# Attention stage: four extra quarters of exponentials, maxima transposed after a group's first quarter, first batch's projection before the last group

## The reference

```python
q, k, v = proj(w_q), proj(w_k), proj(w_v)             # of layernorm(x); (2, 32, 512, 16)
scores = einsum('bhqd,bhkd->bhqk', q, k) / sqrt(16)
attn = softmax(scores, axis=-1)
x = x + einsum('bso,eo->bse', heads(attn @ v), w_o)
x = x + experts(layernorm(x))                          # 2 of 8 experts a token, 800 wide
```

## Time and profile before

| | |
|---|---|
| median of 3 runs | 570.74 us (569.82 to 576.18) |
| the profiled execution | 570.89 us, span 569.0 us |
| TensorE clock granted, mean | 0.986 |
| TensorE busy | 544.3 us, 96% |
| VectorE busy | 390.8 us, 69% |
| ScalarE busy | 323.3 us, 57% |
| attention loop, first V product to last o_raw | 98.6 to 275.7 us |

### The profile page before, as it was taken

One profiled execution on the slowest core, in us unless ns is written; L12 is line 12 of the kernel. 1 busy time (PEld: TensorE's weight loads), 2 busy tenths in 40 slices (PEclk: granted clock), 3 DMA queues, 4 the chain that ended last, 5 costly groups with the idle time before them and its releaser, 6 DMA issues.

```text
span 569.0 us, 9750 instructions
## 1 busy us (share of the span) xinstructions
PE 544.3 (96%) x3504; PEld 394.2 (69%) x3504; DVE 390.8 (69%) x728; ACT 323.3 (57%) x479; POOL 129.3 (23%) x154
## 2 busy tenths in 40 slices
PE   8999999999999999999997999999999999999991
PEld 6886664333333333333766998999999999999991
DVE  6914656999999999961678787663828466576650
ACT  4322114777777777787245473656656575657540
POOL 4300111000230212451301023234240321332202
PEclk9999999999999999999998999999999999999996
DMA  8290367837567752002394878295574757486122
GB/s 327 98 112 0 54 84 87 112 45 89 70 89 90 86 70 88 21 12 87 104 372 169 286 245 290 48 319 110 209 216 140 271 140 291 82 298 169 49 31 36
DMA packets 31116, 78.19 MB, mean 137 GB/s; under 512 B 9692, under 2 KB 10972, under 8 KB 26586
## 3 DMA queue, kind: packets, MB, share of 16 engines
q1 hardware_dynamic: 25770, 68.84, 46.1%
q0 software_dynamic: 5296, 8.69, 8.2%
HBM read 53.11 MB, written 9.32 MB: 110 GB/s over the span
## 4 chain that ended last, share of the span: by engine, by line
PE 79%; DVE 9%; DMA 4%; issue 3%; POOL 2%; ACT 1%; SPq 0%; POOLq 0%; ACTq 0%
PE ps L707 16%; PE ps L709 15%; PE ps L708 15%; PE ps_o L719 9%; PE ps L738 8%; DVE neg_max L1378 6%; PE ps_m L738 4%; DMA q_hi<-o_norm 1%; POOL o_norm L623 1%; PE ps L750 1%; PE ps_m L972 1%; DMA x<-x 1%; PE ps_o L707 1%; PE ps L1007 1%; PE ps L1010 1%
## 5 line engine op out<-in xcount | busy, mean ns | idle before, releaser
L1165 ACT ACTIVATE probs_t<-ps 128x1024 f32<-128x1024 f32 x128 | 124.0, 1022 | 42.0 <-PE ps L750 42.0
L1378 DVE TENSOR_REDUCE neg_max<-ps 128x1 f32<-128x512 f32 x171 | 111.7, 684 | 10.4 <-PE ps L738 7.9
L707 PE MATMUL ps<-xgT_hi,w_hi 128*128 128x256 f32 (+7 forms) x384 | 110.7, 288 | 1.2 <-DVE xgT_lo L1636 1.2
L708 PE MATMUL ps<-xgT_lo,w_hi 128*128 128x256 f32 (+7 forms) x384 | 109.7, 286 | 0.0
L709 PE MATMUL ps<-xgT_hi,w_lo 128*128 128x256 f32 (+7 forms) x384 | 109.7, 286 | 0.0
L738 PE MATMUL ps<-k_stack,q_stack 48*128 48x512 f32 x171 | 72.9, 461 | 2.9 <-issue 0.6
L707 PEld LDWEIGHTS ps<-xgT_hi,w_hi 128*128 128x128 f32 x384 | 72.7, 189 | 1.8 <-DVE xgT_lo L1636 1.6
L708 PEld LDWEIGHTS ps<-xgT_lo,w_hi 128*128 128x128 f32 x384 | 72.7, 189 | 0.1
L709 PEld LDWEIGHTS ps<-xgT_hi,w_lo 128*128 128x128 f32 x384 | 72.7, 189 | 0.0
L719 PE MATMUL ps_o<-probs_t,v_ones 128*32 128x512 f32 x512 | 68.2, 605 | 0.0
L1653 DVE TENSOR_TENSOR act<-gate,ps 128x256 f32<-128x256 f32 (+7 forms) x48 | 20.7, 431 | 68.2 <-PE ps L709 50.5
(11 more groups left out here) (315 smaller groups left out, 995.5 us busy)
## 6 DMA issues: line engine op xcount, KB each, us to landing
w_sb<-w SPq DMA_DIRECT2D x16, 1024.0 KB
w_sb<-w SPq DMA_DIRECT2D x8, 1536.0 KB
w_sb<-w SPq DMA_DIRECT2D x8, 1152.0 KB
q_stack<-q_hi SPq DMA_DIRECT2D x32, 128.0 KB, 5.4
k_stack<-k_hi SPq DMA_DIRECT2D x32, 128.0 KB, 5.0
q_stack<-q_lo SPq DMA_DIRECT2D x16, 128.0 KB, 4.5
k_stack<-k_lo SPq DMA_DIRECT2D x16, 128.0 KB, 6.1
q_hi<-o_norm SPq DMA_DIRECT2D x16, 128.0 KB, 4.3
```

What stands on the lines that cost most here:

```text
L707: pe.matmul(o, x_hi, w_hi, start=start, stop=False)
L708: pe.matmul(o, x_hi, w_lo, start=False, stop=False)
L1165: a.activation(probs_t[:, kc % 2, 2 * half:2 * half + 2, :], ps4[:, 2 * (n % 2):2 * (n % 2) + 2, :], ACT.Exp, scale=D ** -0.5).then_inc(s_ ...
L1378: v.tensor_reduce(neg_max[:, g % 2, col:col + 1], max_bank(g, u2), AX.X, ALU.max, negate=True).then_inc(s_mx, 1)
```

## The change

The order of the loop on TensorE and ScalarE is now a list `steps` of pairs (a, b): quarter a of the maxima and quarter b of the scores, exponentials and V products. After a = 20, 40, 54 and 55 (`AHEAD`) an extra quarter b without maxima is put in, so b runs up to four quarters, one group, ahead of where it was. When all maxima are issued, the projection of tiles 0 and 1 is done in one piece, with M(15) after its second chunk; tile 2 goes into the last group's quarters, and of tile 3 one half into the gap behind it and one behind the last V product. M(ga-1) is issued after the first quarter of group ga, with its turn behind number 3 (`lead` is TPB = 4). ScalarE copies it behind that quarter's two exponentials, in place of ahead of the third. The shuffle stands behind maximum 8. SyncE issues the reciprocal's copy ahead of those of the maxima. The two matmuls of an even unit of scores are swapped (upper head first).

The lines of the changed kernel are 10 higher on TensorE: key maximum L748, scores L760, V product L729, M L739, projection L717 to L719.

```diff
--- before.py
+++ after.py
@@ -30,6 +30,7 @@
 MT = E + EXTRA
 THIRDS = sum(c > 2 * P for c in CAPS)
 LAST = E - 1
+AHEAD = (20, 40, 54, 55)
 MORE_AT = SUBS * LAST + 2
 NSUB = MORE_AT + 2 * EXTRA
 UNIT = 2 * HC * P
@@ -333,11 +334,20 @@
 
         turns = []
         for s in range(-2, NG):
-            lead = 2 if s < 0 else 6
+            lead = 2 if s < 0 else TPB
             turns += [(s + 2, u2) for u2 in range(lead)]
             turns += [(s + 1, "maxima")] * (s + 1 >= 0)
             turns += [(s + 2, u2) for u2 in range(lead, 4 * TPB)]
         turns = [t for t in turns if t[0] < NG]
+
+        steps, b = [], 0
+        for a in range(TPB * (NG - 2)):
+            steps.append((a, b))
+            b += 1
+            if a in AHEAD:
+                steps.append((None, b))
+                b += 1
+        steps += [(None, None)] + [(None, n) for n in range(b, TPB * NG + 2)]
 
         turns += [(t, "projection") for t in range(TPB)] + [(t, "router") for t in range(NT)]
         max_banks = [ps2[:, 0, :], ps2[:, 1, :], ps_m[:, :]]
@@ -460,6 +470,12 @@
                                          frm[HALF * par:HALF * (par + 1), pair, :].bitcast(f32)).then_inc(s_stack[at], 16)
 
             for s in range(-4, NG + 2):
+                g = s - 2
+                if 0 <= g < NG:
+                    sp.wait_ge(s_rc, g + 1)
+                    if g >= 1:
+                        sp.wait_ge(s_sh, g)
+                    sp.dma_start(rec_row[1:P:2 * D, :], sum_rec[:, g % 2, :]).then_inc(s_rb, 16)
                 g = s + 1
                 if 0 <= g < NG:
                     sp.wait_ge(s_mr, g + 1)
@@ -468,12 +484,6 @@
                         sp.dma_start(qs[(g // 2) % RING][row:row + 1, 2 * (g % 2):2 * (g % 2) + 2, :].bitcast(f32)
                                      .rearrange("a p (t c) -> a (p t) c", c=P),
                                      max_rows[8 * par:8 * par + 8, g % 2, :].bitcast(f32)).then_inc(s_row[g % 4], 16)
-                g = s - 2
-                if 0 <= g < NG:
-                    sp.wait_ge(s_rc, g + 1)
-                    if g >= 1:
-                        sp.wait_ge(s_sh, g)
-                    sp.dma_start(rec_row[1:P:2 * D, :], sum_rec[:, g % 2, :]).then_inc(s_rb, 16)
                 g = s - 1
                 if 0 <= g < NG:
                     sp.wait_ge(s_or, g + 1)
@@ -737,7 +747,7 @@
                 max_bank_free(pe, g, u2)
                 pe.matmul(max_bank(g, u2), q[:, qt * P:(qt + 1) * P], k, start=True, stop=True).then_inc(s_sn, 1)
 
-            def scores(g, u):
+            def scores(g, u, order):
 
                 if not 0 <= g < NG:
                     return
@@ -745,7 +755,7 @@
                 if n >= 2:
                     pe.wait_ge(s_ex, n - 1)
                 kc, half = divmod(u, 2)
-                for c in range(2):
+                for c in order:
                     q, k = head_at(g, 2 * half + c, ROWS + 1)
                     last = pe.matmul(ps4[:, 2 * (n % 2) + c, :], k[:, kc * P:(kc + 1) * P], q, start=True, stop=True)
                 last.then_inc(s_st, 1)
@@ -822,35 +832,41 @@
                     max_bank_free(pe, t, "projection")
                 project(max_bank(t, "projection"), t, c0, c1)
 
-            for s in range(0, NG + 1):
-                ga = s + 2
-                if ga < NG and ga % 2 == 0:
+            for a, b in steps:
+                if b is None:
+                    projection(0, 0, HC // 2)
+                    max_t(NG - 1)
+                    projection(0, HC // 2, HC)
+                    projection(1, 0, HC)
+                    continue
+                ga, pa = (NG, 0) if a is None else (2 + a // TPB, a % TPB)
+                s, p = divmod(b, TPB)
+                if a is not None and pa == 0 and ga % 2 == 0:
                     pe.wait_ge(s_stack[(ga // 2) % RING], 16 * 12 * (ga // 2 // RING + 1))
-                if 0 <= s < NG:
+                if p == 0 and s < NG:
                     pe.wait_ge(s_row[s % 4], 32 * (s // 4 + 1))
 
-                for p in range(TPB):
-                    no_pv = 2 - p if s == 0 and p < 2 else 0
-                    key_max(ga, 4 * p)
-                    keep_warm(ps_o, no_pv)
-                    key_max(ga, 4 * p + 1)
-                    keep_warm(ps_o, no_pv)
-                    if p < 2:
-                        pv(s - 1, p + 2)
-                    else:
-                        pv(s, p - 2)
-                    if p == 1 and s + 1 < NG:
-                        max_t(s + 1)
-                    key_max(ga, 4 * p + 2)
-                    scores(s, 2 * p)
-                    keep_warm(ps_o, no_pv)
-                    key_max(ga, 4 * p + 3)
-                    scores(s, 2 * p + 1)
-                    keep_warm(ps_o, no_pv)
-                    if s in (NG - 2, NG - 1):
-                        projection(s - (NG - 2), p, p + 1)
-                    elif s == NG and p == 0:
-                        projection(2, 0, HC // 2)
+                no_pv = 2 - p if s == 0 and p < 2 else 0
+                key_max(ga, 4 * pa)
+                keep_warm(ps_o, no_pv)
+                key_max(ga, 4 * pa + 1)
+                keep_warm(ps_o, no_pv)
+                if p < 2:
+                    pv(s - 1, p + 2)
+                else:
+                    pv(s, p - 2)
+                key_max(ga, 4 * pa + 2)
+                scores(s, 2 * p, (1, 0))
+                keep_warm(ps_o, no_pv)
+                key_max(ga, 4 * pa + 3)
+                scores(s, 2 * p + 1, (0, 1))
+                keep_warm(ps_o, no_pv)
+                if a is not None and pa == 0:
+                    max_t(ga - 1)
+                if s == NG - 1:
+                    projection(2, p, p + 1)
+                elif s == NG and p == 0:
+                    projection(3, 0, HC // 2)
 
             def turned(t):
 
@@ -894,8 +910,7 @@
                                      start=(c == 0), stop=(c == HC - 1))
                 return last
 
-            projection(2, HC // 2, HC)
-            projection(3, 0, HC)
+            projection(3, HC // 2, HC)
             pe.wait_ge(s_ex, UNITS * NG)
             project(ps4[:, 0, :], TPB, 0, HC - 1)
             project(ps4[:, 1, :], TPB + 1, 0, HC - 1)
@@ -1144,8 +1159,12 @@
                 if n >= nj and (1, 2) in between[n - nj]:
                     maxima(0)
 
-            for s in range(0, NG + 1):
-                for u in range(UNITS):
+            for at, b in steps:
+                if b is None:
+                    maxima(NG - 1)
+                    continue
+                s, p = divmod(b, TPB)
+                for u in (2 * p, 2 * p + 1):
                     g = s - 1
                     if u == 2 and g >= 0:
                         a.wait_ge(s_pv, TPB * (g + 1))
@@ -1153,8 +1172,6 @@
                             a.wait_ge(s_so[g % 2], 16 * (g // 2))
                             a.wait_ge(s_on, g - 1)
                         a.activation(o_raw[:, g % 2, :], ps_o[:, :], ACT.Copy).then_inc(s_or, 1)
-                    if u == 2 and s + 1 < NG:
-                        maxima(s + 1)
                     if 0 <= s < NG:
                         n = s * UNITS + u
                         kc, half = divmod(u, 2)
@@ -1164,6 +1181,8 @@
                         a.wait_ge(s_st, n + 1)
                         a.activation(probs_t[:, kc % 2, 2 * half:2 * half + 2, :], ps4[:, 2 * (n % 2):2 * (n % 2) + 2, :],
                                      ACT.Exp, scale=D ** -0.5).then_inc(s_ex, 1)
+                if at is not None and at % TPB == 0:
+                    maxima(1 + at // TPB)
 
             def turned(t):
 
@@ -1446,7 +1465,7 @@
                         elif s == NG + 1:
                             scaled(xn2, x1, 0, 2, s_xn2)
                             residual(2)
-                    if u2 == 11 and g >= 0:
+                    if u2 == 8 and g >= 0:
                         v.wait_ge(s_rb, 16 * (g + 1))
                         if g >= 1:
                             v.wait_ge(s_on, g)
```

## The result

| | before | after | forecast |
|---|---|---|---|
| median | 570.75 us | 579.79 us (579.07 to 580.30) | 580.0 |
| after / before | | 1.0148, interval 1.0112 to 1.0183 | 1.016 |
| profiled execution (span) | 570.89 (569.0) | 579.82 (578.1) | 580.1 |
| last maximum starts | 250.56 | 263.60 | 263.0 |
| last o_raw starts | 275.06 | 285.43 | 284.6 |

Slower by 1.5%, 9.0 us, where +9.3 was forecast. The intervals between the starts of the "a" maxima on VectorE are the length of a quarter. For one group they read 2.91, 2.71, 3.03, 2.69 before and 3.30, 3.03, 2.69, 2.70 after; over an extra quarter 4.53 (at 20) and 4.49 (at 40); with a row wait 4.07, 4.03 and, before the last extra quarters, 4.54.

The account below looks back on a forecast made before the run. It took a loop through three PSUM banks for maxima and the V product, 2.71 us a quarter, as the bound, not any engine's load. Terms: 570.9 + 12.4 - 2.9 - 0.3 = 580.1, stated as 580.0, range 572.5 to 586.

Parts of the forecast that it names:

- The loop: Maximum on VectorE, freed PSUM bank, next maximum, V product, next maximum: 0.69 + 0.06 + 0.43 + 0.99 + 0.54 = 2.71 us a quarter.
- M's bank wait: First quarter of a group: matmul 5 waits for number 3's bank, 3.30 in place of 2.91 us, 12 x 0.38 = 4.6.
- The rival without a bank wait: Transpose M's place costs nothing and M leaves the loop: 7.1 us less, 573.0; chance 0.15.
- Extra quarters: Quarters without key maxima at 20, 40, 54: V product stays on the loop, +1.55, +1.55, +1.35 us, sum 4.4.
- Row waits: TensorE waits for the row of maxima before the first quarter of groups 12, 13, 14: +1.1 us each, 3.4.
- rows in time: Rival at groups 12 to 14: without the 3.4 us of waits for rows of maxima, 576.7 us; chance 0.12.
- late rows: Rival: rows of maxima behind busy DMA engines, up to 2.8 us in place of 1.1 each, 585 us; chance 0.05.
- The tail: Last maximum to last o_raw: 21.6 us in place of 24.5, so -2.9; four quarters at 2.55 make 10.2.
- The last chain: Copies behind the last V product, from last o_raw to projection, 12.0 us: -0.3 expected, bounds 0 to -0.7.
- its queue is a bit less pushed: Last rec_row copy, issued 0.7 us after its reciprocal, may come earlier as its queue is less pushed: -0.3 us.
- The shuffle and the scores' order: Shuffle behind maximum 8 still makes a 3.03 us quarter, costed at 0; swapped score matmuls cost the same either way.

Follow-up runs that it names:

- both shorter loops: Two runs on the kernel before: transpose M moved behind key maximum 6, 571.24 us (0.9984); VectorE's shuffle split in two halves, 569.81 us (0.9970).
- the run of M alone: Kernel before with only the transpose of the maxima (M) and its copy moved behind a group's first quarter: 574.77 us, 1.0068.
- the run with it at full clock: Changed kernel with the second extra quarter at 53 in place of 40: 576.97 us, 1.0113 against the kernel before.
- the two runs on the row wait: Changed kernel with ScalarE's copy of M between that quarter's two exponentials, 576.74 us; changed kernel with the second extra quarter at 53, not 40, 576.97 us.
- M behind 6: Kernel before with transpose M behind key maximum 6 and its bank turn behind number 6: 571.24 us, 0.9984.
- both edits: Kernel before with transpose M behind key maximum 6 and the shuffle in two halves, behind maxima 11 and 15: 570.98 us, 0.9995.

## Why the prediction was right, step by step

*The loop* held. Each of its five links can be found in the timeline of after, and both shorter loops came out of it.

*M's bank wait:* forecast 12 x 0.38 = 4.6. Measured 0.39 in 11 quarters, and next to nothing (0.02) in the first, which is longer for other reasons: 4.3. The rival without a bank wait (573.0) fell with the run of M alone.

*Extra quarters:* forecast 1.55, 1.55 and 1.35; measured 4.53 - 2.91 = 1.62, 4.49 - 2.91 = 1.58, and 1.35 for the third in the run with it at full clock (4.05 - 2.70). Sum 4.55 against 4.4.

*Row waits:* forecast 1.1 each, measured 4.07 - 3.03 = 1.04, 1.00, and 4.54 - 3.03 = 1.51 for the third. The row was forecast 5.1 behind the a in front of M; that a is one quarter of 3.30 ahead of the one at 228.05, and the row is there at 229.74, so 4.99 behind it; the third is there 5.48 behind (250.22 to 255.70). Sum 3.55 against 3.4. The rivals with rows in time and late rows fell.

*The half clock* was no term of mine: 4.93 in place of 4.05, 0.88 us. The expectations of the two runs on the row wait put 1.35 on it; 0.47 of that was the longer third row wait. This is what the sum lacked. The terms above come to 4.3 + 4.55 + 3.55 = 12.4, the 12.4 of the forecast; with the 0.88 they are 13.28, and the last maximum moved by 13.04. Of the 0.24 between, 0.07 is an earlier start, and most of the rest is 0.02 in each group: the quarter with the shuffle and the one without are together 5.72 in place of 5.74.

*The tail:* 21.83 against 21.6; the four quarters are 10.22 (10.2).

*The last chain:* forecast -0.3, measured -0.83, outside my bound of -0.7. The step "its queue is a bit less pushed" was the right direction and the wrong mechanism: the copy waited behind the store of the group before, and all of that wait went, not a part of it. In the kernel before M's place frees it by itself (10.20), and so does SyncE's order together with the shuffle's place (10.11).

*The shuffle and the scores' order* at nothing: right. The group stays 11.34 with the shuffle behind maximum 8 (tested together with SyncE's order), and 570.45 against 571.04 is no difference for the scores.

Sum by the profile: 13.04 - 2.67 - 0.83 = 9.54, and behind the chain 0.5 less (281.5 in place of 282.0 us; in both kernels the clock is low for some stretches of 3.4 us there, not the same ones), together 9.03, the difference of the spans. The forecast was 12.4 - 2.9 - 0.3 = 9.2. Its errors of +0.6, +0.2, -0.5 and -0.5 cancel, and that is luck: by its terms it was good to about half a us each, not to the 0.2 of the total.

## What to carry to other kernels

When no engine is full, look for the loop through a rotating buffer (here: maximum, free bank, matmul, V product, next maximum) and price an edit by what it does to that loop. An insertion costs nothing only where the loop waits anyway, and one that takes a turn in the rotation shifts everybody's wait by a turn: the same transpose cost 0.21 us a group behind number 5, 0.6 behind number 3 and less than 0.1 behind number 6. And a thin stretch of TensorE can cost time behind it at half clock (0.88 us behind a stall of 1.75, 2.65 in the first step), so that a shorter order may come out no faster until its first steps are kept busy.

## What the runs showed of the hardware

- TensorE's clock fell to half behind one stall of 1.75 us, for 3.41 us, and didn't behind two shorter ones of the same kind (the first two row waits, 1.26 and 1.22), nor in the runs that shortened this stall or took it away. In the first step, with M moved by one key maximum, it fell for 6.83 us in one profiled execution (M behind 6) and not in another (both edits).
- A shuffle of 128x512 holds VectorE for 0.63 us (the next maximum starts so much behind it) and one of 128x256 for 0.34, so the two halves cost 0.05 us more than the whole.
- The order of the row halves in the scores made no difference that can be measured (570.45 against 571.04), and none in the timeline.
